# Attention of a decoder layer on one core: pieces six slots apart, banks swapped, values grouped 3, 6, 4, output in two halves

## What is computed

```python
q = (x @ Wq).reshape(b, n, HEADS, DIM_HEAD).transpose(0, 2, 1, 3)
k = (context @ Wk).reshape(b, m, HEADS, DIM_HEAD).transpose(0, 2, 1, 3)
v = (context @ Wv).reshape(b, m, HEADS, DIM_HEAD).transpose(0, 2, 1, 3)
scores = jnp.einsum('bhnd,bhmd->bhnm', q, k) * scale
attn = jax.nn.softmax(scores, axis=-1)
out = jnp.einsum('bhnm,bhmd->bhnd', attn, v)
out = out.transpose(0, 2, 1, 3).reshape(b, n, HIDDEN)
return out @ Wo + bo
```

## Time and profile before

| | us |
|---|---|
| median of 3 runs | 963.65 |
| lowest and highest | 959.42, 964.48 |
| the profiled execution's own time | 962.75 |
| its span, first to last instruction | 960.5 |
| mean granted clock of TensorE, share of full | 0.981 |

### The profile page before, as it was taken

How to read it: one execution, slowest core, us unless ns; L and a number is a source line. 1 busy time by engine, 2 the same in 40 slices (tenths; PEclk the granted TensorE clock), 3 DMA queues, 4 the chain that set the end, 5 groups by cost and what they waited for, 6 DMA issues and landing times. The chain is left out here.

```text
span 960.5 us, 13006 instructions
## 1 busy us (share of the span) xinstructions
PE 910.0 (95%) x4616; PEld 537.4 (56%) x4616; DVE 554.3 (58%) x1123; ACT 351.4 (37%) x493; POOL 592.2 (62%) x397
## 2 busy tenths in 40 slices
PE   6998799999999999999999999999799999989993
PEld 2655354555565455555555465545578888855552
DVE  2897556667647667657667647644645121136562
ACT  2245244434335444425444425443341111124332
POOL 0453198888877888868888868893104400038885
PEclk9999899999999999999999999999799999999997
DMA  8013200000001000001000001040597100423310
GB/s 269 27 49 116 99 1 1 23 1 1 1 1 44 23 1 2 1 1 45 23 1 1 1 1 45 1 154 1 140 324 254 50 22 22 124 78 111 92 38 16
DMA packets 42873, 52.85 MB, mean 55 GB/s; under 512 B 4400, under 2 KB 33856, under 8 KB 42816
## 3 DMA queue, kind: packets, MB, share of 16 engines
q1 hardware_dynamic: 35808, 44.21, 14.7%
q0 software_dynamic: 3744, 6.32, 2.1%
q10 hardware_dynamic: 3264, 1.57, 0.6%
HBM read 38.42 MB, written 17.59 MB: 58 GB/s over the span
## 5 line engine op out<-in xcount | busy, mean ns | idle before, releaser
L600 POOL TENSOR_TENSOR accG<-accG,probs 128x1024 f32<-128x1024 f32 (+1 forms) x170 | 404.0, 2377 | 52.0 <-ACT probs L623 30.1
L623 ACT ACTIVATE probs<-st 128x1024 f32<-128x1024 f32 (+1 forms) x208 | 211.3, 1026 | 207.1 <-PE st L784 195.4
L667 DVE TENSOR_REDUCE mxp<-mx 128x1 f32<-128x512 f32 x360 | 231.6, 686 | 85.2 <-PE mx L770 79.0
L806 PE MATMUL av<-probs,V 128*64 128x512 f32 (+1 forms) x832 | 188.4, 596 | 0.0
L770 PE MATMUL mx<-K_hi,Q_hi 64*128 64x512 f32 (+1 forms) x480 | 164.0, 391 | 6.0 <-DVE mxp L667 4.5
L806 PEld LDWEIGHTS av<-probs,V 128*64 128x64 f32 (+1 forms) x832 | 56.8, 137 | 106.1 <-issue 100.6
L770 PEld LDWEIGHTS mx<-K_hi,Q_hi 64*128 64x128 f32 x480 | 78.9, 184 | 66.4 <-DVE mxp L667 34.5
L784 PE MATMUL st<-Q_hi,K_hi 64*128 64x512 f32 (+1 forms) x416 | 109.1, 440 | 0.9 <-ACT probs L623 0.9
L784 PE MATMUL st<-M,ones_r 64*128 64x512 f32 (+1 forms) x416 | 108.0, 394 | 0.0
L784 PE MATMUL st<-Q_hi,K_lo 64*128 64x512 f32 (+1 forms) x416 | 102.5, 391 | 0.0
L784 PE MATMUL st<-Q_lo,K_hi 64*128 64x512 f32 (+1 forms) x416 | 102.0, 390 | 0.0
(11 more groups left out here) (198 smaller groups left out, 1196.5 us busy)
## 6 DMA issues: line engine op xcount, KB each, us to landing
w_gate_up<-in_gate_up SPq DMA_DIRECT2D x4, 2048.0 KB, 20.8
w_down<-in_down SPq DMA_DIRECT2D x2, 2048.0 KB, 15.9
xs<-scratch_sorted_x SPq DMA_DIRECT2D x31, 128.5 KB, 2.1
scratch_sorted_x<-zero SPq DMA_DIRECT2D x7, 514.0 KB, 8.6
xT<-in_xT SPq DMA_DIRECT2D x4, 512.0 KB, 6.6
xring<-in_x SPq DMA_DIRECT2D x4, 512.0 KB, 9.4
scratch_x1b<-xT SPq DMA_DIRECT2D x4, 512.0 KB, 2.9
x<-scratch_x1b SPq DMA_DIRECT2D x4, 512.0 KB, 3.9
```

Of the source, the lines that this page charges most:

```text
L600: pool.tensor_tensor(total[0:r], so_far[0:r], probs[0:r, place(S, t)], ALU.add).then_inc(g_add, 1)
L623: act.activation(probs[0:r, place(S, t)], st[g % 2][0:r, :], ACT.Exp, scale=DH ** -0.5).then_inc(a_probs, 1)
L667: dve.tensor_reduce(mxp[:, F % 2, h * QT + i, j:j + 1], mx[h][:, 0:kn], AX.X, ALU.max).then_inc(v_mx, 1)
L806: mm = pe.matmul(av[h * DH:(h + 1) * DH, :], V[0:r, t, (2 * p + h) * DH:(2 * p + h + 1) * DH], probs[0:r, place(S, t), h * QC:(h + 1) * QC ...
```

## The change

- **Banks.** The query's projection goes to `misc` (before `mx0`), the transposed maxima go to `mx1` (before `misc`). The projection's wait becomes one for the divisions two steps back, and piece 1 waits for Q_hi alone and no more for Q_lo; the `sums` wait for Q_lo, which reads `misc`.
- **Pieces.** Head 0's pieces stand six slots apart from tile 1 on, head 1's one slot behind; the short pair moves from the end to tile 9 (`SHORT`), and a whole pair stands between the values of tiles 9 and 10 (`LATE_PAIR`).
- **Values.** The tiles are run 5, 4, 4 as before, the values after them are 3, 6, 4 (`VALUES`).
- **Divisions.** Two after maximum 8 and two after maximum 16 (before three and one).
- **Output.** Its first half (`misc`) stays ahead of the last values, its second half (`mx0`) comes after them; residuals 0 and 1 stand ahead of the last two maxima, 2 and 3 after them.
- **GpSimd** waits for two exponentials at once at most tiles (`SEEN`).

The diff, cut to its core:

```diff
-PIECE_AT = {1: (4, 4), 2: (3, 4), 3: (4, 4), 4: (4, 4), 5: (0, 2), 6: (1, 3), 7: (2, 4), 8: (3, 4),
-            9: (0, 2), 10: (1, 3), 11: (2, 4), 12: (3, 4)}
-DIVIDE_AFTER = (8, 8, 8, 16)
+VALUES = (range(0, 3), range(3, 9), range(9, KT))
+PIECE_AT = {1: (0, 1), 2: (1, 2), 3: (2, 3), 4: (3, 4), 5: (0, 1), 6: (1, 2), 7: (2, 3), 8: (3, 4),
+            9: (0, 1), 10: (0, 1), 11: (1, 2), 12: (2, 3)}
+SHORT = 8
+LATE_PAIR = 10
+DIVIDE_AFTER = (8, 8, 16, 16)
+SEEN = {3: 4, 5: 6, 7: 8, 9: 10, 11: 12}
...
-                    pool.wait_ge(a_probs, S * KT + t + 1)
+                    if shared or t not in SEEN.values():
+                        pool.wait_ge(a_probs, S * KT + (t if shared else SEEN.get(t, t)) + 1)
...
+                        if n == PIECES - 2 and p == 0 and c > 0:
+                            residual(c - 1, 0, misc)
+                            residual(c - 1, 1, misc)
                     all_maxima(S + 1)
                     if p == 0 and c > 0:
-                        for i in range(QT):
-                            residual(c - 1, i, misc if i < 2 else mx[1])
+                        residual(c - 1, 2, mx[0])
+                        residual(c - 1, 3, mx[0])
...
             def max_transpose(S):
                 at_least(pe, v_nm, S)
-                at_least(pe, v_o, (S - 1) * DIVS)
-                c, p = divmod(S - 1, PAIRS)
-                if S > 0 and p == 0 and c > 0:
-                    pe.wait_ge(v_r, (c - 1) * QT + 2)
-                pe.transpose(misc[:, 0:P], nm[:, S % 2], ident[:]).then_inc(p_mT, 1)
+                pe.transpose(mx[1][:, 0:P], nm[:, S % 2], ident[:]).then_inc(p_mT, 1)
...
             def q_proj(F):
                 c, pair = divmod(F, PAIRS)
-                at_least(pe, v_mx, (F - 1) * PIECES)
+                at_least(pe, v_o, (F - 2) * DIVS)
+                if pair == 2 and c > 0:
+                    pe.wait_ge(v_r, (c - 1) * QT + 2)
...
-                    mm = pe.matmul(mx[0][:], wq[:, k, pair * P:(pair + 1) * P], x1T[:, k, :],
+                    mm = pe.matmul(misc[:], wq[:, k, pair * P:(pair + 1) * P], x1T[:, k, :],
...
                 if n == 1:
-                    pe.wait_ge(v_lo, F)
+                    pe.wait_ge(a_hi, F)
...
+                if n <= 2:
+                    at_least(pe, v_mx, (F - 2) * PIECES + PIECES - 2 + n)
...
+                    at_least(pe, v_lo, S + 2 if S + 2 < STEPS else 0)
...
-                for run in RUNS:
+                for run, given in zip(RUNS, VALUES):
                     for t in run:
                         tile(S, t, n if ahead and t in PIECE_AT else None)
                         n += 2 if t in PIECE_AT else 0
                     if run is RUNS[0] and S > 0:
                         sums(S - 1)
-                    if run is RUNS[-1]:
-                        if ahead:
+                    if run is RUNS[-1] and p == 0 and c > 0:
+                        output(c - 1, 0)
+                    for t in given:
+                        if t == LATE_PAIR and ahead:
                             piece(S + 1, n)
                             piece(S + 1, n + 1)
-                        if p == 0 and c > 0:
-                            output(c - 1)
-                    for t in run:
                         values(S, t)
+                if p == 0 and c > 0:
+                    output(c - 1, 1)
```

More of the change, by code:

```diff
@@ L535, in piece_of @@
             whole = len(MC) - 1
-            return (None, whole) if k == PIECE_PAIRS - 1 else (k // whole, k % whole)
+            if k == SHORT:
+                return None, whole
+            return (k - (k > SHORT)) // whole, (k - (k > SHORT)) % whole
         block = ctx.enter_context(nc.Block())
@@ L606, in q_high @@
                 at_least(act, p_qk, 2 * (F - 1) * KT)
-                act.activation(Q_hi[F % 2][:], mx[0][:], ACT.Copy).then_inc(a_hi, 1)
+                act.activation(Q_hi[F % 2][:], misc[:], ACT.Copy).then_inc(a_hi, 1)
             def exp(S, t):
@@ L651, in max_rows @@
                 dve.wait_ge(p_mT, S + 1)
-                dve.tensor_tensor(M[:].rearrange("p (i q) -> p i q", i=QT), misc[:, 0:P].unsqueeze(1).to_broadcast([P, QT, P]),
+                dve.tensor_tensor(M[:].rearrange("p (i q) -> p i q", i=QT), mx[1][:, 0:P].unsqueeze(1).to_broadcast([P, QT, P]),
                                   mask[:].unsqueeze(2).to_broadcast([P, QT, P]), ALU.mult).then_inc(v_mT, 1)
@@ L656, in q_low @@
                 dve.wait_ge(a_hi, F)
-                dve.tensor_tensor(Q_lo[F % 2][:], mx[0][:], Q_hi[F % 2][:].bitcast(F32), ALU.subtract).then_inc(v_lo, 1)
+                dve.tensor_tensor(Q_lo[F % 2][:], misc[:], Q_hi[F % 2][:].bitcast(F32), ALU.subtract).then_inc(v_lo, 1)
             def piece_maximum(F, n):
@@ L824, in sums, with output @@
                 mm.then_inc(p_sum, 1)
[L826 to L833, removed]
+            def output(c, half):
+                if half == 0:
+                    pe.wait_ge(d_wo, 16)
+                    pe.wait_ge(v_o, (c + 1) * PAIRS * DIVS)
+                else:
+                    pe.wait_ge(v_mx, ((c + 1) * PAIRS + 1) * PIECES)
+                bank = (misc, mx[0])[half]
+                for i in (2 * half, 2 * half + 1):
                     for p in range(PAIRS):
```

## The result

| | before | after |
|---|---|---|
| time, median of 4 runs | 962.82 us (959.42 to 964.48) | 940.03 us (938.92 to 940.72) |
| profiled execution: time | 962.75 | 938.92 |
| its span | 960.5 | 937.1 |
| first to last transpose (the attention) | 529.6 | 509.1 |
| ahead of the first transpose | 108.9 | 108.1 |

The ratio is 0.977, with an interval of 0.9751 to 0.9789: faster by 2.3%, 22.8 us between the medians. The forecast was 946 in a range of 940 to 958.

The account below looks back on a forecast made before the run. TensorE's own queue, stopped by waits for maxima and exponentials, was taken as the bound. Terms summed to -1.27 us a step, -19.0 over fifteen steps, +1.6 after outputs: -17.4, so 946 us, range 940 to 958.

Parts of the forecast that it names:

- Tiles 0 to 4: Start of a step, first score to sums: earlier pieces cut 7.00 us to 6.26, -0.74 a step.
- Tiles 5 to 8: Second run of tiles in a step: 5.30 us against 5.33, -0.03 a step.
- thin margins: Tiles 5 to 8: pieces 14 and 16 find banks free by under 0.05 us; between 0 and +0.25 if this fails.
- Values regrouped: Values 3, 6, 4: two values move from the first gap to the second, both still ending in one switch; 0.
- their cover: Gaps of the values hide the divisions on VectorE; without them each would hold up a maximum by 1.2 us.
- Tiles 9 to 12: Last run of tiles, short passes now in tile 9, taken as 1.73 us: 5.78 against 6.85, -1.07 a step.
- The late pair: Whole pair between values 9 and 10, two more switches of TensorE's shape: +0.57 us a step.
- Output in two halves: Three steps after an output: late residuals delay M and maximum 1, tiles 0 to 4 take 6.8 us; +0.53 each.
- (a): Rival: VectorE sets the pace, three more 0.25 us delays a step stay; -0.52 a step, 957 us; chance 0.13.
- (b): Rival: late pieces lengthen the exponential's round trip in all three runs of every step; slower, 970 us; chance 0.05.
- (c): Rival: the late pair's maxima or residuals hold up transpose or M about a microsecond; 961 us; chance 0.06.
- (d): Rival: shorts wholly covered, next tile's loads pulled across a late piece; -1.75 us a step, 938 us; chance 0.12.

## Why the prediction was right, and where its sizes were off

**What bounds the kernel.** Right. TensorE's queue with its two waits gave every segment. ScalarE is on the path only with the round trip of an exponential, and GpSimd isn't on it; undoing its merged waits changed nothing.

**Tiles 0 to 4, -0.74.** Right: -0.72 in the changed kernel, -0.71 alone, +0.71 when undone (6.99). The hand count holds inside the run too: tile 3 at 3.62 after tile 0 (318.20, counted 3.61), head 1's late piece at 4.46 (counted 4.56), tile 4 at 4.93 (319.51, counted 5.02), the sums at 6.28 (counted 6.26). The two that are 0.10 early are passes that restart: their records are 0.49 and 0.50 long instead of 0.39 and contain the restart, which the count put ahead of them.

**Tiles 5 to 8, -0.03.** +0.02, so the thin margins held.

**Values regrouped, 0.** Right as a move of values (509.7 against 509.1). What I named as their cover is shown by the three divisions in one gap: 0.57 of loss in tiles 5 to 8, half of the 1.2 that I had put for a division without cover, since the gap still hid a part of it.

**Tiles 9 to 12, -1.07.** The sign and place right, the size off: -1.30. **The step that failed is the price of the short passes in tile 9.** From "four shorts are 0.58 where the score beside them is 0.23, so each head adds 0.35" I added 0.35 once for each head and put tile 9 at 1.73. It took 1.48 (335.09 to 336.57). Four slots and a restart are 1.03 of it, so the eight short passes added 0.45 and not 0.70. The 0.58 was near: head 1's four took 0.56 alone in the kernel before, and all eight take 0.57 side by side. What failed is to add up the two heads. I had read 1.15 as eight passes that run one after another; there head 1's four had waited for a maximum, and where they don't, they run beside head 0's: in tile 9 head 1's first starts, by the individual records, at 335.45 with head 0's last. This term is short by 0.23 a step over tiles 9 to 12 (5.78 against 5.55), 3.5 us over fifteen steps, and is more than the whole difference in the attention (3.0); smaller terms on both sides make up the rest (below). The other part of the loss there, piece 24 late by 0.25, was counted rightly: the two kernels that remove it gain 0.22.

**The late pair, +0.57.** Right: 0.58 by the segments, and shown again by the kernel that puts the pair ahead of the values (3.59 for the last four values, 4.17 with the pair between them). The Trainium skill (TensorEngine Tiling (Array Packing), Key Properties) says that a change of mode drains TensorE, which had led me to weigh 0.1 more. It is not there: 12.47 became 13.05, and by that sum it would be 13.14.

**Output in two halves, +0.53 three times.** Too much: tiles 0 to 4 take 0.20 more there, and the step as a whole 0.15 (32.35 for 32.20). I had taken the 3.04 from M's start to Q_lo's end out of the earlier trace rows; it is 2.85 now. In the kernel before Q_lo waited for Q_hi (on ScalarE from 290.01 for 0.60, Q_lo from 290.64); in the changed one Q_hi is written by 282.88, well ahead of Q_lo at 283.32. A wait lay inside this price too. And the maximum starts 0.08 before Q_lo's end, where I had put it behind it. 0.4 us instead of 1.6, a gain over the forecast of 1.1. Where both output halves were left together, there was no lateness at all (32.91 beside 32.93). No run tests the divided output by itself, but nothing here shows a gain from it.

**The sum.** -17.4 forecast, -20.4 measured. Step by step: eight ordinary steps give 1.435 each, the three with an output 1.35, the three after one 1.25, the first 1.15: 11.48 + 4.06 + 3.74 + 1.15 = 20.4. The 3.0 over the forecast are 3.5 at tile 9 and 1.1 in the steps after an output, less 0.5 in the first step and those with an output, and less fifteen times the 0.05, 0.02 and 0.01 that tiles 5 to 8, tiles 0 to 4 and the late pair came out dearer than counted (1.2); that is 2.9, and 3.0 up to rounding. The profiled execution is 23.8 us shorter (938.92 for 962.75). Of this 20.4 are attention, 2.9 lie ahead of it (0.8) and behind it (2.1), and 0.45 outside the span. Outside the attention the change does nothing by itself, and two profiles of the same kernel differ there by 3.3. So of the 6 us by which the time is under the forecast only about half is shown to belong to the change. What differs can be seen at the attention's end. Stretches of 15 us there, before and after: us, busy time of each engine, granted clock, DMA share, GB/s:

```profile
675.00:690.00 15.00, 11.46 (x36) 7.44 (x35) 11.36 (x33) 5.55 (x14) 2.66 (x9) 0.66 0.37 112
```

```profile
654.00:669.00 15.00, 10.49 (x41) 6.90 (x41) 12.18 (x36) 6.39 (x16) 2.66 (x9) 0.89 0.46 133
```

TensorE has the same sparse work in both, waiting for the last divisions, and the granted clock falls towards the lower level of 1.2 GHz for longer in the first (0.66 against 0.89 on average). But the kernel with only the first five tiles changed also shows 0.66 there and spends the shortest time but two of all thirteen profiles after its last transpose (319.3; all lie from 318.5 to 322.0). So the clock is not enough to tell these 2.9 us, and I leave them open.

**The rivals.** (a), VectorE sets the pace, did not come true: in an ordinary step two slots between the heads win nothing in tiles 0 to 8. One of its three delays is real, the 0.22 in tiles 9 to 12, and the forecast had that one in its sum. (b) did not happen; tile 11 starts 2.79 after its run's start (337.88), just under the 2.8 that I had put as its mark. The mark was a bad one, since the forecast itself had tile 11 at 3.13. What speaks against (b) is that no run of tiles took over 0.05 more than counted. (c) did not happen: the late pair's maxima end ahead of the transpose, which comes 2.73 after the last values' start, those three values' own length (three times 0.86 and a change of shape). (d), "shorts wholly covered", is half true: 0.22 of tile 9 stay uncovered, and the forecast and (d) share what came out, 940 between 938 and 946.

## What to carry to other kernels

Where two producers share one slow consumer, count the second one's bank through: its distance from the first has to cover what the first holds the consumer for, or the delay has to fall on something that would wait anyway. A delay at the end of a run, with no such wait behind it, is paid in full; that was 3.4 us for one slot in the last run of tiles. Before the length of a row is taken as a price, look whether a wait lies inside it: eight passes read 1.15 us in one place and 0.57 in another. And before two prices are added, look whether the two can run side by side.

## What was not expected of the hardware

- Short passes of both heads (66 columns each) run side by side at 0.11 us a pair when both banks are free, half the slot of a full pass (0.23).
- VectorE starts an operation 0.57 to 0.60 us after the one before it where each takes 0.65 to 0.69, also across kinds: a subtraction (283.32), then a maximum (283.89).
- A change of TensorE's shape and back costs 0.58 with a pair in between, of which 0.43 is the pair's own stretch; no drain beyond it shows.
- The record of a pass that restarts after a wait is 0.49 to 0.50 us long instead of 0.39 to 0.40 (319.04, 319.51): the 0.10 of the restart lies in the record.
